# Low rows stored before the wait for B and C, and all six carry copies given to ScalarE

## What is computed

```python
# per image, for the forward and the reversed sequence
xr, z = split(layernorm(x) @ W_in)
xr = silu(causal_conv4(xr))                    # 192 channels
dbl = xr @ W_xproj                             # low-rank dt, B and C (16 states each)
dt = softplus(dbl[..., :6] @ W_dt + b_dt)
def step(h, inp):                              # h is 192 x 16 per pixel
    h = exp(dt_t[:, :, None] * A) * h + (dt_t * x_t)[:, :, None] * B_t[:, None, :]
    return h, einsum("ben,bn->be", h, C_t)
y = (ys + xr * D) * silu(z) @ W_out
out = (out_fwd + out_rev) * 0.5 + x
```

## Time and profile before

| | us |
|---|---|
| median of three runs | 5679.4 (5677.27 to 5689.04) |
| the profiled execution | 5688.73 |
| its span | 5686.9 |
| first scan starts at | about 217 |
| busy in the span | DVE 5250.7, POOL 5083.4, PE 4461.4, ACT 4314.0 |
| mean granted clock of TensorE | 0.83 |

### The profile page before, as it was taken

One profiled execution on the slowest core, in us unless ns is written; L12 is line 12 of the kernel. 1 busy time (PEld: TensorE's weight loads), 2 busy tenths in 40 slices (PEclk: granted clock), 3 DMA queues, 4 the chain that ended last, 5 costly groups with the idle time before them and its releaser, 6 DMA issues.

```text
span 5686.9 us, 47026 instructions
## 1 busy us (share of the span) xinstructions
PE 4461.4 (78%) x12946; PEld 1313.2 (23%) x12946; DVE 5250.7 (92%) x4449; ACT 4314.0 (76%) x6863; POOL 5083.4 (89%) x1737
## 2 busy tenths in 40 slices
PE   8877887778877888778887788777887778876676
PEld 3222222222222222222222222222222222221121
DVE  2799999999999999999999999999999999999998
ACT  3577777877787877878777777777777777777665
POOL 0599999999999999999899999999999999999998
PEclk7888888788887888788888888888888788887778
DMA  4576776777776776777777777776777677777776
GB/s 113 119 179 163 176 176 164 171 178 168 177 173 161 175 177 163 174 171 169 173 173 167 173 172 168 171 176 159 175 175 167 163 176 174 169 172 166 170 175 155
DMA packets 417567, 954.66 MB, mean 168 GB/s; under 512 B 56624, under 2 KB 56873, under 8 KB 382744
## 3 DMA queue, kind: packets, MB, share of 16 engines
q1 hardware_dynamic: 417304, 951.65, 70.8%
HBM read 770.08 MB, written 181.36 MB: 167 GB/s over the span
## 4 chain that ended last, share of the span: by engine, by line
DVE 22%; DMA 18%; POOL 18%; PE 16%; ACT 13%; issue 9%; SPq 4%; POOLq 0%; DVEq 0%; ACTq 0%
DVE X L1389 15%; POOL X L1497 12%; DMA bc_d<-bc 5%; POOL X L1486 5%; DVE X L1372 4%; PE ps L765 3%; PE ps L744 3%; ACT ps L1096 3%; DMA lo_d<-bc 3%; DMA out<-xf 3%; DMA hi_d<-S 3%; DMA lo<-lo_d 2%; PE ps L799 2%; DMA xf<-x_d 2%; ACT hid L982 1%
## 5 line engine op out<-in xcount | busy, mean ns | idle before, releaser
L1497 POOL TENSOR_TENSOR X<-X,cR 128x2048 f32<-128x2048 f32 x768 | 3473.6, 4527 | 64.3 <-ACT carry L1101 32.1
L1389 DVE TENSOR_TENSOR_SCAN X<-ps,carry,X 128x512 f32<-128x512 f32 x2688 | 3263.4, 1260 | 157.7 <-ACT ps L1096 157.6
L1096 ACT ACTIVATE ps<-hi,amat 128x512 f32<-128x512 f32 x2048 | 1376.0, 682 | 669.5 <-DVE X L1389 666.0
L799 PE MATMUL ps<-X,red 128*32 128x512 f32 x6144 | 912.4, 671 | 487.0 <-POOL X L1497 485.9
L1486 POOL TENSOR_TENSOR X<-lo,bR 128x2048 f32<-128x2048 f32 x258 | 1168.4, 4529 | 127.0 <-DMA lo<-lo_d 126.1
L1372 DVE TENSOR_TENSOR X<-hi,ps 128x2048 f32<-128x2048 f32 x512 | 1158.3, 2262 | 35.4 <-PE ps L799 30.1
L765 PE MATMUL ps<-win,w_u 97*128 97x512 f32 (+1 forms) x2080 | 1144.4, 702 | 3.4 <-ACT xr L1052 0.9
L1096 ACT ACTIVATE ps<-lo,amat 128x512 f32<-128x512 f32 x1026 | 691.1, 682 | 133.8 <-DVE X L1389 119.9
L780 PE MATMUL ps<-xr,wd 128*96 128x512 f32 (+1 forms) x520 | 433.4, 930 | 306.6 <-ACT xr L1052 249.6
L765 PEld LDWEIGHTS ps<-win,w_u 97*128 97x128 f32 (+1 forms) x2080 | 383.8, 195 | 682.9 <-issue 678.5
L1389 DVE TENSOR_TENSOR_SCAN X<-ps,X 128x512 f32<-128x512 f32 x384 | 445.3, 1202 | 34.5 <-ACT ps L1096 34.4
(11 more groups left out here) (125 smaller groups left out, 3842.1 us busy)
## 6 DMA issues: line engine op xcount, KB each, us to landing
hi<-hi_d SPq DMA_DIRECT2D x516, 512.0 KB, 8.0
bR<-bc_d SPq DMA_DIRECT2D x516, 256.0 KB, 4.6
lo<-lo_d SPq DMA_DIRECT2D x516, 256.0 KB, 4.6
cR<-bc_d SPq DMA_DIRECT2D x516, 256.0 KB, 7.2
hi_d<-S SPq DMA_DIRECT2D x258, 256.0 KB, 8.4
y_d<-yf SPq DMA_DIRECT2D x128, 256.0 KB, 10.2
yb<-y_d SPq DMA_DIRECT2D x112, 256.0 KB, 10.0
win<-xn_d SPq DMA_DIRECT2D x130, 195.1 KB
```

The costliest lines, as they stand in the source:

```text
L799: last = mm(p_y[GRP * j:GRP * j + GRP, :], red[:, :], X[:, slot(par, s), j, :], start=False, stop=(s in (LOW - 1, NB - 1)), skip_group_che ...
L1096: A_(p_a[i % RING][:, :], dt, ACT.Exp, scale=amat[:, column(i):column(i) + 1]).then_inc(s_exp, 1)
L1389: V.tensor_tensor_scan(h, a, h, 0.0 if head else carry[:, i:i + 1], ALU.mult, ALU.add).then_inc(s_scan, 1)
L1497: G.tensor_tensor(batch(par, s), batch(par, s), quads(cR, par, s), ALU.mult).then_inc(s_hc, 1)
```

## The change

`BY_SCALAR` now has all six batches, so `BY_POOL` is empty: GpSimd copies no carry, and ScalarE copies one at each of the steps 4, 8, 12, 16, 20 and at step 0 of the next body (before: 4, 16 and 0). `store_low` stands directly behind `store_bc`.

```diff
-        BY_SCALAR = (0, 3, NB - 1)
+        BY_SCALAR = tuple(range(NB))
         BY_POOL = tuple(s for s in range(NB) if s not in BY_SCALAR)
...
                 store_bc(n + 1, nxt)
+                store_low(n + 1, nxt)
                 if fin and rev:
                     load_y(0, (img + 1) * NCH, chunk_of(q, rev, odd), n * NB + (LOW + 2))
                 load_b(n + 1, nxt)
-                store_low(n + 1, nxt)
                 sp.wait_ge(s_exp, n * NT + LOW * BATCH)
                 load_low(n + 1, nxt)
...
-                    if i in (4, 16):
+                    if i > 0 and i % BATCH == 0:
                         keep_carry(n, i // BATCH - 1, par, rev)
```

## The result

The change makes the kernel slower: median 5941.6 us (5928.2 to 5948.5, four runs) against 5678.3 us, a ratio of 1.0464 with a 95% interval of 1.0446 to 1.0483. The forecast was 5800 us and its range ended at 5895. The direction and the place were right. The forecast growth of 120 us was less than half of the true one, 263 us.

A forecast was written before the change was run, and what follows sets the result against it. A ring through GpSimd, TensorE, ScalarE and VectorE, not one full engine, was taken as the bound. Per pair 3.8 + 0.1 - 1.85 = 2.05 us, over 58 pairs 119 us, gave 5800 us; range 5680 to 5895.

The forecast's parts named there:

- Parts 1 and 3: GpSimd's dropped carry copies save 0.27 us per body before product 4; earlier low-row stores give back 2.0 us per pair.
- GpSimd's piece: Stretch from product 2's start to product 5's end; savings of 2.0, 0.5 and 0.5 us per pair were forecast.
- the lateness: Time from scan 11's end to product 2's start; product 2 was forecast 6.8 us later per pair of bodies.
- Part 2: Product 2 waits for ScalarE's carry behind the Gelu group: 4.4 us later in even bodies, 2.4 us in odd.
- The slack: Idle time behind product 5 absorbing delay: 2.4 us in odd forward, 1.3 in even reverse bodies, mean 1.85 per pair.
- part 4: ScalarE's added carry copy at step 8, in front of the Gelu group in even bodies, costs 0.1 us per pair.
- the way back: Stretch from product 5's end to the next body's scan 11 end, forecast to absorb 1.85 us per pair.
- A: GpSimd relieved, product 5 comes earlier and ScalarE's waits shrink, so the kernel is faster, 5585 us; chance 0.14.
- B: Slack everywhere: GpSimd's 370 us of waits absorb the delay, no change, 5680 us; chance 0.09.
- C: No slack behind product 5, delay goes through in full, TensorE's projection and Silu group also held: 5906 us; chance 0.12.
- The signs: Profile after: 400 to 560 us idle before product 2, low-row wait at most 20 us, last 12 bodies unaffected.

The follow-up runs named there:

- e1: The change with the low-row stores put back in their old place, all six carries still on ScalarE: 5954.6 us, ratio 1.0472.
- e9: The change, with TensorE's expert tiles 1 and 2 made in front of sum 1 in reverse bodies: 5923.0 us, ratio 1.0438.
- e7: The change, with TensorE's expert products 3 to 5 and the bias moved in front of product 5's sum: 5963.3 us, ratio 1.0491.
- e11: The change, with TensorE making expert tile 3 twice between sums 4 and 5 in odd bodies: 5937.8 us, ratio 1.0466.
- e2: The kernel before the change with only the low-row stores moved early, carries divided as before: 5595.6 us, ratio 0.9844.
- e5: The change, with batch 2's carry kept before the second table load and exponential 14 in Gelu-group bodies: 5732.9 us, ratio 1.0082.
- e6: The change, with batch 2's carry kept one step later, behind exponential 15: 6116.0 us, ratio 1.0754.

## Why the prediction was right, and where it failed

**Parts 1 and 3** hold. GpSimd's piece was forecast to shrink by (2.0 + 0.5 + 0.5) / 2 = 1.5 us per body and did by 29.00 - 27.57 = 1.43. The stores follow the low dt x at once, the residual's wait is 6.4 us. That the low rows' saving and the lateness cover each other is shown by e1. Its residual wait of 13.7 us says that the earlier residual, too, needs no moved stores once product 2 is late.

**Part 2** names the right mechanism and undersizes it. Forecast: 3.4 us later per body. Measured: 4.30 - 0.35 = 3.95. By kinds, even forward bodies gave 4.60 and odd ones 2.82 and 2.57, near the 4.4 and 2.4 read from bodies 52 and 53. Even reverse ones, of which I had read none, gave 5.81. I had read the Gelu group where it stood before the change. Product 1's lateness, which I had put down as covered, moved the group itself in even reverse bodies (e9 takes 1.0 us of it back there), and in odd forward ones the third Gelu waits too (0.41 us at 2606.69).

**The slack** is the step that failed. I counted 1.85 us per pair, 0.93 us per body less 0.05 for part 4, that the way back would give. It gave 13.32 - 13.13 = 0.19. By kinds: for odd forward bodies I had counted 2.4 and they gave 12.07 - 11.19 = 0.88; for even reverse ones 1.3, and they gave 0.41; even forward bodies, where I had found none, took 0.46 more. The term thus measured (0.88 - 0.46 + 0.41 - 0.04) / 2 = 0.40 per pair in place of 1.85.

Part of the error was the reading. Body 53's 3.0 us of idle time is not typical: the mean over the 29 odd forward bodies, up to exponential 13, was 1.8 us, of which 0.7 were left after the change. The rest is successors that I didn't price. TensorE, which stands longer in front of sum 5, does it at the granted clock of 0.50 in all 57 odd bodies, where it was 0.50 in 21 of them and 1.00 in 28 before. It takes 1.94 us, for 1.67 in forward and 1.23 in reverse ones before. In even forward bodies the x2 wait grew from 1.78 to 2.44 us (22 bodies that follow a forward one). In the 21 even reverse bodies that follow a reverse one, where the residual's wait was to be won, it fell from 1.26 to 0.32 us, and the wait for x2 behind it grew from 0.12 to 1.17: "where a stall goes, say what is late next" is the question that I had answered for the low rows only. What each of these successors is worth is read from the traces; e7 and e11, which take two of them away, gain nothing in sum, since each puts sum 5 back in some bodies.

In numbers: the missing lateness, 0.55 us, and the missing slack, 0.88 - 0.19 = 0.69 us, with 0.07 less given back, are 1.31 x 116 = 152 us on top of 119. That makes 271, and measured are 263. The closeness is in part luck: in the profiled executions, 246.8 us apart, the first 116 bodies grew by 266 us, while the head before the first scan became 13.5 us shorter and the last 12 bodies 5.6.

**Rivals.** A fell: GpSimd was relieved and the kernel slowed. A saving exists, though: e2 measured -88 us for the low rows without the moved carries. That this is near the -96 of that rival's working is chance, since those 96 counted the copies too and halved the sum. The Trainium skill says to optimise the engine of highest occupancy first (Perfetto Trace Analysis, Identifying the Most-Contended Engine). Read as "take instructions off a nearly full engine", it fails here: GpSimd's busy share fell by 5 points and the time rose by 4.6%. The engine of highest occupancy was VectorE (92%), though, so this case doesn't test the rule as it is written. B fell by e5 and e6. C, "no slack, and more", with 5906 us and a chance of 0.12, was the nearest; it should have been the forecast, and the range should have gone past it. What C missed is mostly the lateness of even reverse bodies; the cause that it named, TensorE's projection and the Silu group, no run here singles out.

**The signs** I had set came out but for the last: 559 us of idle in front of product 2 (400 to 560 forecast; the 724.9 us also hold 164 us in front of product 1), over 2 us in each of the first 116 bodies, low rows' wait under 20 us, the low stores 0.03 us behind the low dt x, 768 carries. In the last 12 bodies I had expected nothing of it. Yet product 2 is late there too, 0.93 us behind scan 11 for 0.48 before; since GpSimd's piece shrank by 1.3 us, these bodies still got a little shorter (41.2 us each for 41.7, from the first scan of body 116 to the end of the last).

## What to carry to other kernels

When a small step moves to another in-order engine, don't ask how busy that engine is but what stands in front of the step there at the moment when it is due; here a 0.19 us copy behind 4.4 us of Gelu and table loads cost 2.3 us in every body. If the step lies on a ring, take the full delay as the forecast, and count an idle time as slack only after taking its mean over all bodies of its kind, walking on from it, and pricing what would be late next. Try a two-part change in its parts: the half with the stores alone is worth 1.6%, and nothing of it showed in the whole.

## What was unexpected in the hardware

With the low stores moved up, the landing of transfers of unchanged size took longer: low loads 7.8 us for 4.6, high stores 11.6 us for 8.4, C loads 10.7 us for 7.2, in e2, which is faster than the kernel before. e1, with all carries moved and the stores in their old place, has 4.7, 8.3 and 7.3 us, so it is the moved stores that do it. They bring the transfers closer together on the one queue: from the issue of the last B load to that of the first low load it was 6.2 us before (median) and is 0.5 us in e2. The landing is counted from the issue; that the loads share the DMA engines and so land later is my reading and wasn't tested. The low rows, for which GpSimd stood 126.1 us before, are waited for only 17.3 us in e2 in spite of it.
